# Angle attention's node state and table in five parts at the head of each pass, and layer norms in five parts on ACT and DVE

## The reference

```python
h = relu(layernorm(x));  x = x + weighted_means(h)      # L0
h = relu(layernorm(x));  x = x + graph_conv_with_experts(h)   # L1
h = relu(layernorm(x));  x = x + angle_attention(h)     # L2, four passes
h = relu(layernorm(x));  x = x + graph_attention(h)     # L3, three passes

def layernorm(x):                     # over the 256 features, no gain and no shift
    m = mean(x); v = var(x)
    return (x - m) / sqrt(v + 1e-5)

def agnn_layer(h, src, dst, beta):    # one pass of L2, a relu behind each
    h_norm = h * rsqrt(sum(h * h) + 1e-16)
    logits = beta * sum(h_norm[src] * h_norm[dst])
    ex = exp(logits - segment_max(logits, dst)[dst])
    alpha = ex / (segment_sum(ex, dst)[dst] + 1e-16)
    return segment_sum(alpha * h[src], dst)
```

## Time and profile before

| what | value |
|---|---|
| median of 3 runs | 10534.61 us (10525.16 to 10535.69) |
| the profiled execution's own time | 10475.0 us |
| its span, from the first to the last instruction | 10473.3 us |
| busy: PE, DVE, ACT, POOL | 61%, 49%, 29%, 52% of the span |
| angle attention | from about 3992 to 7501 us |
| mean granted TensorE clock | 0.823 of full speed |

### The profile page before, as it was taken

How to read it: one execution, slowest core, us unless ns; L and a number is a source line. 1 busy time by engine, 2 the same in 40 slices (tenths; PEclk the granted TensorE clock), 3 DMA queues, 4 the chain that set the end, 5 groups by cost and what they waited for, 6 DMA issues and landing times. The chain is left out here.

```text
span 10473.3 us, 149576 instructions
## 1 busy us (share of the span) xinstructions
PE 6360.4 (61%) x33521; PEld 5067.1 (48%) x33705; DVE 5160.9 (49%) x13884; ACT 2997.1 (29%) x7335; POOL 5395.9 (52%) x5498
## 2 busy tenths in 40 slices
PE   0004334434453954885787788678568867776876
PEld 0003324433343843664665566466445545554554
DVE  7002223341113226555556555555667757775777
ACT  0000000000001212333333333333245545553554
POOL 2766666646652123554554555455255545563554
PEclk9996666666676977998998899899788888898888
DMA  3201113343343952334334334333333343342334
GB/s 134 73 8 40 39 40 86 86 58 99 92 72 119 364 185 63 82 83 72 83 82 70 86 82 82 73 81 83 47 85 76 78 68 73 77 79 65 79 76 68
DMA packets 615211, 886.77 MB, mean 85 GB/s; under 512 B 285857, under 2 KB 423587, under 8 KB 613834
## 3 DMA queue, kind: packets, MB, share of 16 engines
q0 software_dynamic: 241344, 609.84, 26.8%
q1 hardware_dynamic: 373770, 275.99, 8.7%
HBM read 757.80 MB, written 134.33 MB: 85 GB/s over the span
## 5 line engine op out<-in xcount | busy, mean ns | idle before, releaser
L1569 POOL DMA_INDIRECT hs<-tab_agnn,rec x1952 | 1877.0, 962 | 1700.9 <-issue 535.0
L2010 POOL DMA_INDIRECT hs<-tab_gat,rec x1464 | 1514.7, 1035 | 1135.7 <-DVE msg L2084 522.1
L1633 DVE CUSTOM_DVE_ANT_0 prod<-psG,hs 128x256 f32<-128x256 f32 x1952 | 836.0, 482 | 992.2 <-remote 528.1
L1692 PE MATMUL psG<-HN,ohT 128*128 x3904 | 1103.9, 428 | 94.4 <-DVE lg L1633 76.8
L2042 DVE TENSOR_REDUCE mt<-psL 128x2 f32<-128x1024 f32 x732 | 871.9, 1219 | 463.8 <-remote 245.0
L1709 PE MATMUL psV<-hs,pr 128*128 128x258 f32 x3904 | 1005.4, 404 | 2.9 <-DVE acc L1616 2.8
L1692 PEld LDWEIGHTS psG<-HN,ohT 128*128 128x128 f32 x3904 | 779.1, 212 | 241.8 <-DVE lg L1633 102.0
L2175 PE MATMUL psV<-msg,oh 128*128 128x260 f32 x2928 | 821.1, 429 | 16.1 <-issue 13.8
L1709 PEld LDWEIGHTS psV<-hs,pr 128*128 128x128 f32 x3904 | 758.0, 205 | 103.7 <-DVE acc L1616 4.4
L661 PE MATMUL psT<-ident,oh 128*128 128x128 f32 x488 | 120.0, 393 | 1128.4 <-issue 792.6
L1648 ACT ACTIVATE prT<-cand,mn 128x512 f32<-128x512 f32 x488 | 352.4, 722 | 1485.8 <-DVE mn L1594 1091.4
(11 more groups left out here) (320 smaller groups left out, 12565.0 us busy)
## 6 DMA issues: line engine op xcount, KB each, us to landing
w<-in_L_gnn_w SPq DMA_DIRECT2D x224, 512.0 KB, 5.7
fwd_d<-acc SPq DMA_DIRECT2D x10, 3172.0 KB
fw<-fwd_d SPq DMA_DIRECT2D x122, 260.0 KB
hs<-tab_agnn,rec POOLq DMA_INDIRECT x1952
hs<-tab_gat,rec POOLq DMA_INDIRECT x1464
rec<-rec_d SPq DMA_DIRECT2D x1220, 8.0 KB
b<-in_L_gnn_b SPq DMA_DIRECT2D x113, 128.0 KB, 6.5
x<-xbuf SPq DMA_DIRECT2D x112, 128.0 KB, 6.2
```

Of the source, the lines that this page charges most:

```text
L1569: nc.gpsimd.indirect_dma_start(out=hs[:, j, g, :], out_offset=None, in_=k.tab_agnn, in_offset=bass.IndirectOffsetOnAxis(ap=rec[:, j, g, 0: ...
L1633: ins = V.tensor_tensor_reduce(prod[:, h2, g, :], psG[:, bank(j2, half), m, :], hs[:, j2, g, 0:D], hs[:, j2, g, D:D + 1], 0.0, ALU.mult, A ...
L1692: mm = nc.tensor.matmul(psG[:, bank(j1, half), m, :], ohT[:, j1 % 2, 2 * half + m, :], pick(HN, b, slice(None)).rearrange("p a c -> p (a c ...
L2010: nc.gpsimd.indirect_dma_start(out=hs[:, j, g, :], out_offset=None, in_=k.tab_gat, in_offset=bass.IndirectOffsetOnAxis(ap=rec[:, j, g, 0:1 ...
```

## The change

The layer norm's instructions are cut into five parts of five blocks each, and DVE and ACT work at different parts at a time. The subtraction of the mean is gone as a sweep of its own: ACT squares `X - mean` with the mean as its bias, one instruction per block (25 of 256 columns), and DVE makes `(X - mean) * rstd` in one instruction per block with both as scalars. The norm can write somewhere else than into `k.H`.

In angle attention the head and the tail of a pass are no blocks of their own any more. What the tail did for the state, and what the head did for the norm, the table and `HN`, stands in front of each engine's part of the pipeline, in five parts. The product and the maximum with 0 are one instruction. `k.acc` and `low` are cleared by POOL, a part of `k.acc` when DVE has read it. SP stores the table in five parts and goes on to the records without waiting; POOL waits for all five before it gathers, and PE for all of `HN`. The layer norm ahead of angle attention writes into `k.acc`, with ones as the sum of exponentials, so that the first pass begins as the others do. Behind the fourth pass the state is made once more in front of the addition to `k.X`.

```diff
@@ class Norm
+        self.root = sb("root", [P, NB], F32)
     def on_vector(self, dve):
-        c = Chain(dve, q.ln, n * 6)
-        Hf = k.H[:, :, 0:D]
-        c.done(nc.vector.tensor_reduce(mean[:, :], k.X[:, :, :], AX.X, ALU.add))
-        c.done(nc.vector.tensor_scalar(mean[:, :], mean[:, :], 1.0 / D, None, ALU.mult))
-        c.done(nc.vector.tensor_tensor(Hf, k.X[:, :, :], b3(mean[:, :], D), ALU.subtract))
-        dve.wait_ge(q.ln_sq, n + 1)
-        c.done(nc.vector.tensor_reduce(var[:, :], sq[:, :, :], AX.X, ALU.add))
-        c.done(nc.vector.tensor_scalar(var[:, :], var[:, :], 1.0 / D, LN_EPS, ALU.mult, ALU.add))
+        for c in range(NORM_PARTS + 1):
+            if c < NORM_PARTS:
+                V.tensor_reduce(mean[:, norm_part(c)], k.X[:, norm_part(c), :], AX.X, ALU.add).then_inc(q.ln_sum, 1)
+            if c >= 1:
+                dve.wait_ge(q.ln_sum, n * NORM_PARTS + c)
+                V.tensor_scalar(mean[:, norm_part(c - 1)], mean[:, norm_part(c - 1)], -1.0 / D, None, ALU.mult).then_inc(q.ln_mean, 1)
+        for c in range(NORM_PARTS):
+            dve.wait_ge(q.ln_sq, n * NORM_PARTS + c + 1)
+            ins = V.tensor_reduce(var[:, norm_part(c)], sq[:, norm_part(c), :], AX.X, ALU.add)
+        c = Chain(dve, q.ln, n * 3)
+        c.done(ins)
+        c.done(V.tensor_scalar(var[:, :], var[:, :], 1.0 / D, LN_EPS, ALU.mult, ALU.add))
         dve.wait_ge(q.ln_sd, n + 1)
-        c.done(nc.vector.reciprocal(rstd[:, :], mean[:, :]))
-        nc.vector.tensor_tensor(sq[:, :, :], Hf, b3(rstd[:, :], D), ALU.mult).then_inc(q.ln_h, 1)
+        c.done(V.reciprocal(rstd[:, :], root[:, :]))
+        for c in range(NORM_PARTS):
+            for b in range(NB)[norm_part(c)]:
+                ins = V.tensor_scalar(sq[:, b, :], k.X[:, b, :], mean[:, b:b + 1], rstd[:, b:b + 1], ALU.add, ALU.mult)
+            ins.then_inc(q.ln_out, 1)
     def on_scalar(self, act):
-        act.wait_ge(q.ln, n * 6 + 3)
-        nc.scalar.activation(sq[:, :, :], k.H[:, :, 0:D], ACT.Square).then_inc(q.ln_sq, 1)
...
+        for c in range(NORM_PARTS):
+            act.wait_ge(q.ln_mean, n * NORM_PARTS + c + 1)
+            for b in range(NB)[norm_part(c)]:
+                ins = nc.scalar.activation(sq[:, b, :], k.X[:, b, :], ACT.Square, bias=mean[:, b:b + 1])
+            ins.then_inc(q.ln_sq, 1)
+        act.wait_ge(q.ln, n * 3 + 2)
+        nc.scalar.activation(self.root[:, :], var[:, :], ACT.Sqrt).then_inc(q.ln_sd, 1)
+        for c in range(NORM_PARTS):
+            act.wait_ge(q.ln_out, n * NORM_PARTS + c + 1)
+            nc.scalar.activation(self.to[:, norm_part(c), 0:D], sq[:, norm_part(c), :], ACT.Relu).then_inc(q.ln_h, 1)
@@ def attention_by_angle
-    layernorm(nc, k)
+    layernorm(nc, k, k.acc)
...
+                nc.vector.memset(k.acc[:, :, D + 1], 1.0)
...
-            with nc.Block() as block:
-
-                @block.scalar
...
+            def state_on_vector(dve):
+                V.tensor_scalar(ss[:, :], k.acc[:, :, D + 1], 1e-16, None, ALU.add).then_inc(s_node, 1)
+                dve.wait_ge(s_node, layer * 2 + 1)
+                V.reciprocal(rn[:, :], ss[:, :]).then_inc(s_node, 1)
+                dve.wait_ge(s_node, layer * 2 + 2)
+                for n in range(NC + 2):
+                    if n < NC:
+                        c = part(n)
+                        V.scalar_tensor_tensor(out=k.H[:, c, 0:D], in0=k.acc[:, c, 0:D], scalar=0.0, in1=b3(rn[:, c], D),
+                                               op0=ALU.max, op1=ALU.mult).then_inc(s_h, 1)
+                    if 1 <= n <= NC:
+                        c = part(n - 1)
+                        dve.wait_ge(s_sq, nc_of(n))
+                        V.tensor_reduce(ssq[:, c], HN[:, c, :], AX.X, ALU.add).then_inc(s_sum, 1)
+                        dve.wait_ge(s_sum, nc_of(n))
+                        V.tensor_scalar(ssq[:, c], ssq[:, c], 1e-16, None, ALU.add).then_inc(s_eps, 1)
+                    if n >= 2:
+                        dve.wait_ge(s_sd, nc_of(n - 1))
+                        V.reciprocal(k.H[:, part(n - 2), D], root[:, part(n - 2)]).then_inc(s_norm, 1)
+                dve.wait_ge(s_norm, nc_of(NC))
+                V.tensor_scalar(rnb[:, :], k.H[:, :, D], betas[:, ds(layer, 1)], None, ALU.mult).then_inc(s_rnb, 1)
+                dve.wait_ge(s_rnb, layer + 1)
+                for n in range(NC):
+                    V.tensor_tensor(HN[:, part(n), :], k.H[:, part(n), 0:D], b3(rnb[:, part(n)], D), ALU.mult).then_inc(s_hn, 1)
+                dve.wait_ge(s_mem, layer * (NC + 1) + (NC + 1))
+
+            def state_on_scalar(act):
+                for n in range(NC + 1):
+                    if n < NC:
+                        act.wait_ge(s_h, nc_of(n + 1))
+                        nc.scalar.activation(HN[:, part(n), :], k.H[:, part(n), 0:D], ACT.Square).then_inc(s_sq, 1)
+                    if n >= 1:
+                        act.wait_ge(s_eps, nc_of(n))
+                        nc.scalar.activation(root[:, part(n - 1)], ssq[:, part(n - 1)], ACT.Sqrt).then_inc(s_sd, 1)
+
+            def state_on_pool(pool):
+                nc.gpsimd.memset(low[:, :], BIG).then_inc(s_mem, 1)
+                for n in range(NC):
+                    pool.wait_ge(s_h, nc_of(n + 1))
+                    nc.gpsimd.memset(k.acc[:, part(n), :], 0.0).then_inc(s_mem, 1)
+                pool.wait_ge(s_tab, nc_of(NC) * 16)
+
+            def state_on_sync(sp):
+                for n in range(NC):
+                    sp.wait_ge(s_norm, nc_of(n + 1))
+                    sp.dma_start(rows(k.tab_agnn[0:NP, :])[:, part(n), :], k.H[:, part(n), 0:W_AGNN]).then_inc(s_tab, 16)
...
                 @block.tensor
                 def _(pe):
+                    pe.wait_ge(s_hn, nc_of(NC))
...
-            with nc.Block() as block:
-
-                @block.vector
-                def _(dve):
-                    c = Chain(dve, s_end, layer * 4)
...
+                c.done(V.scalar_tensor_tensor(out=HN[:, :, :], in0=k.acc[:, :, 0:D], scalar=0.0, in1=b3(rn[:, :], D),
+                                              op0=ALU.max, op1=ALU.mult))
+                c.done(V.tensor_tensor(k.X[:, :, :], k.X[:, :, :], HN[:, :, :], ALU.add))
```

More of the change, by code:

```diff
@@ L451, in on_scalar, with layernorm @@
         sq, mean, var = self.sq, self.mean, self.var
-        act.wait_ge(q.ln, n * 6 + 3)
-        nc.scalar.activation(sq[:, :, :], k.H[:, :, 0:D], ACT.Square).then_inc(q.ln_sq, 1)
[L454 to L460, removed]
+        for c in range(NORM_PARTS):
[8 more added lines that the diff above has]
+            nc.scalar.activation(self.to[:, norm_part(c), 0:D], sq[:, norm_part(c), :], ACT.Relu).then_inc(q.ln_h, 1)
+def layernorm(nc, k, to=None):
     with ExitStack() as ctx:
-        norm = Norm(nc, k, lambda n, s, d: ctx.enter_context(nc.sbuf_tensor(tagged(nc, n), s, d)))
+        norm = Norm(nc, k, lambda n, s, d: ctx.enter_context(nc.sbuf_tensor(tagged(nc, n), s, d)), to)
         with nc.Block() as block:
@@ L1460, in attention_by_angle @@
         rn = sb("rn", [P, NB])
+        ssq = sb("ssq", [P, NB])
+        root = sb("root", [P, NB])
         rnb = sb("rnb", [P, NB])
@@ L1504, in _ @@
                 nc.vector.memset(k.H[:, :, D + 1:W_AGNN], 1.0)
+                nc.vector.memset(k.acc[:, :, D + 1], 1.0)
+        NC = 5
+        part = lambda n: slice(n * (NB // NC), (n + 1) * (NB // NC))
         with nc.Fori(0, L2_LAYERS) as layer:
-            with nc.Block() as block:
-                @block.scalar
[L1510 to L1513, removed]
-                @block.vector
-                def _(dve):
[L1517 to L1520, removed]
-                    c.done(nc.vector.tensor_reduce(ss[:, :], HN[:, :, :], AX.X, ALU.add))
-                    c.done(nc.vector.tensor_scalar(ss[:, :], ss[:, :], 1e-16, None, ALU.add))
-                    dve.wait_ge(s_sq, layer * 2 + 2)
-                    c.done(nc.vector.reciprocal(k.H[:, :, D], rn[:, :]))
-                    c.done(nc.vector.tensor_scalar(rnb[:, :], k.H[:, :, D], betas[:, ds(layer, 1)], None, ALU.mult))
-                    c.mark(nc.vector.tensor_tensor(HN[:, :, :], k.H[:, :, 0:D], b3(rnb[:, :], D), ALU.mult))
-                @block.sync
-                def _(sp):
-                    sp.wait_ge(s_node, layer * 5 + 3)
-                    sp.dma_start(rows(k.tab_agnn[0:NP, :]), k.H[:, :, 0:W_AGNN]).then_inc(s_tab, 16)
-                    sp.wait_ge(s_tab, layer * 16 + 16)
@@ L1720, in _ @@
                     pipeline(pe, step, 5, numbers=blocks)
-            with nc.Block() as block:
-                @block.vector
-                def _(dve):
-                    c = Chain(dve, s_end, layer * 4)
-                    V = nc.vector
-                    c.done(V.tensor_scalar(ss[:, :], k.acc[:, :, D + 1], 1e-16, None, ALU.add))
-                    c.done(V.reciprocal(rn[:, :], ss[:, :]))
-                    c.done(V.tensor_tensor(HN[:, :, :], k.acc[:, :, 0:D], b3(rn[:, :], D), ALU.mult))
```

(11 more changed lines are left out.)

33 lines of the change are left out of this document (29 added, 4 removed).

## The result

The changed kernel took 10423.06 us (median of 4 runs, 10392.32 to 10437.46) against 10533.26 of the kernel before in the same session (4 runs, 10525.16 to 10535.69): ratio 0.989, 95% interval 0.9862 to 0.9918, so 110 us faster. The forecast was 10425. The two profiled executions differ by only 51.6 us in span: the one of the kernel before took 10475.0, 58 us under its median, the one of the kernel after 10423.42, at its median, and 40 us of the gap lie in the four loops.

The account below looks back on a forecast made before the run. No engine bounds the whole span; the work is a chain of phases. Savings of 45 + 5.5 + 49.8 + 2.0 + 7.3 = 109.6 us, taken from the median 10534.6, gave 10425, range 10385 to 10478.

Parts of the forecast that it names:

- The norms: Three exposed layer norms: 24.5 us each instead of 39.7, taken as 15 saved each, 45 in all.
- The first norm: Norm beside POOL's scatter of records: 5.5 us from ending long scatters; 11.7 more for POOL, or nothing if DMA sets the pace.
- The heads: Starts of the angle attention passes: 16.6 us saved in each of three, 49.8 in all, and 2.0 in the first.
- E to S: From the end of a pass's last accumulation to DVE's first instruction of the next head: 4.9 us instead of 19.5.
- the step that put its start behind HN: First gather of a pass: POOL could start at S+22.3, but HN's two-input instructions put it at S+24.3.
- PE's new wait: PE's wait for HN in the head: holds back only first transposes, which need oh, behind HN on DVE; no cost.
- The fill: Pipeline filling after a pass's first gather: stays 33 us long and shifts with the heads.
- rival B: DVE pauses before the first oh: up to 16.6 us lost in three heads, 10 in the first; 10485; chance 0.17.
- Rival C: No DVE pause in the fill: up to 15 us more saved in three heads; 155 in all, 10380; chance 0.12.
- The tail: After the last angle attention pass: one DVE sweep (6.82) and a barrier (0.48) go, 7.3 us saved.
- Rival D: Angle loops fetch code at each turn, 2.5 us times 76, 190 us: 80 slower, 10615; chance 0.05.
- Rival F: Parts of the heads don't overlap, ACT loading tables twice per part: 5 us a head, 20 in all; 10445; chance 0.05.

Follow-up runs that it names:

- session 1: Follow-up session with four kernels: before 9341.55 us, norms alone ratio 0.9963, heads alone 0.9926, the whole change 9217.63, ratio 0.9865.
- run with one part: Changed kernel with only the first of five parts of HN made, four fifths of the scaled state left out: 9224.28 us, a single run.
- run with the later wait: Changed kernel with PE's wait for HN moved behind its load of block numbers, to the second loop step: 9226.14 us, ratio 0.9873.
- the later wait and HN shared: Changed kernel with PE's wait for HN behind its number loads and ACT making the last two of HN's five parts: 10297.99 us, ratio 0.9895.
- sessions 1 and 2: The first two follow-up sessions; the kernel before took 9341.55 and 9346.38 us in them.
- the first pair: The original profiled executions, kernel before against changed kernel: 10475.0 and 10423.42 us.
- session 3: Follow-up session repeating both kernels unchanged: changed 10295.72 us against 10402.23 before, ratio 0.9888.

## Why the prediction was right, and where it was not

**The norms** (45 forecast) gave 44.1. Two parts were off by more than 0.2 us. The 25 tensor_scalar take 8.17 us, 0.33 each, not the 0.27 of the earlier trace rows; nearer the other bound of the step, 0.34. Of the 1.4 us that this costs, 0.8 came back ahead of it: the five sums with their scalings took 7.5 us, not 8.2, so the first tensor_scalar starts 15.5 us into the norm, not 16.3.

**The first norm** (5.5) gave nothing: the last scatter starts at 716.9 against 716.3. The term's premise was right, POOL did gain; that the gain reaches the end of the scatter was wrong. The scatters of 6.42 and 7.18 us are gone; the line's rows in the kernel after (minimum, median, maximum in ns):
```profile
L415 POOLq MOVE  x392: 29/700/703, 178.7 to 718.3; - x196
L415 POOL DMA_INDIRECT rec_d<-R x392: 969/971/1149, 179.6 to 716.9; - x196
...
  DMA rec_d<-R: 19.1, 4
```
The longest scatter is 1.15 us, but POOL then waits 19.1 us for the scatters' own transfers, where it waited 10.5 before. In session 1 these waits went from 10.9 to 22.6 us, by just the 11.7 that the two long scatters had cost: the transfers set the pace, the step's lower bound. The rule that I weighed there, of the Trainium skill (SBUF — State Buffer, "SBUF: two separate sides"), would have the 25 tensor_scalar lock POOL too. This trace shows next to nothing of it: while they ran, from 200.96 to 209.12, POOL's scatters took 0.99 to 1.06 us, 0.02 to 0.09 more than beside nothing; as each lasts 0.33 us, a hold as short as one of them isn't excluded. What stood beside the long scatters of the earlier trace rows was an instruction with two inputs in SBUF. The same section of the Trainium skill names that form too, against a GpSimd instruction that reads SBUF, so it covers what the prediction took the trace to add. With HN, of that form, the trace agrees: the gather ends 0.8 us after HN's last part, whenever it began.

**The heads** (49.8 and 2.0 forecast) gave 59.8 and 5.3 up to the gather, and gave some of it back behind it. E to S was 3.4, not 4.9: I had taken the jump's cost over whole from the earlier trace rows; it was 1.5 us less a pass, and why, no run tells. The gather came at S+22.7 to S+23.5 by pass and run, not S+24.3: the step that put its start behind HN was wrong. HN holds its end, and that costs 0.5 us, as the run with one part showed. The 5.3 of pass 1 are some 4 us from S on (from S+27.2 to S+23.3) and 1.4 ahead of it.

**PE's new wait** was costed at nothing, "holds back only its first transposes, which need oh". As to when PE starts, that step failed. Behind the wait stands the load of the block numbers, 2.88 us, and then the transposes: 3 us late, of which 1 reaches the product, since the gathered rows come late as well. The run with the later wait shows it: from gather to product its four passes take 30.3 us, after in session 1 33.8 and before 29.0. That is 3.5 of the +4.9 in the table. In the time of the pass it costs nothing where loops take 700 us, for the same table has -4.6 in the next row; where they take 780, it may be what brings the pause forward.

**The fill** was forecast to shift unchanged. It did in session 1, where gather to first accumulation takes 132.3 us in four passes against 132.0. Where loops last 780 us it grew by 10 to 13 us, 5 to 11 of them behind the first product. That is rival B in its direction (DVE pauses earlier), but only a tenth to a fifth of the 60 us that B put on it: in the profile the earlier pause also ends earlier, in mid-burst, and a second, shorter one follows. With the later wait and HN shared this growth was gone. Rival C, no pause, is what sessions 1 and 2 show in both kernels, so it was never the change's to bring.

**The tail** (7.3) gave 7.1.

**Rival D** falls: loops of the same length, and in the kernel after two instruction packets within 5 us at the outer jump (4841 to 4846) and none in 680 us of loop (4973 to 5653), as in the earlier trace rows. The rule of the Trainium skill (Runtime: NRT & Kernel Launch, "Instruction fetch mechanics") that a branch out of the window stalls stays untested: no packet came in the stretch of loop looked at. **Rival F** falls too: ACT loads a table before the first Square and before the first Sqrt of each head and never between the parts.

**The sum** was 109.6. With the rows down to the first accumulation the table gives 102 in the first pair (116.3 - 2.6 - 10.8 - 0.6), 117 in session 1 and 108 in session 3. The medians differ by 110, 124 and 107. So in the session of the forecast the term that came out too small (the heads, by 13) and those that came out too large or were missed (the first norm 5.5, PE's load and the fill 13) nearly cancel: the mechanism of the big terms was right, the closeness to 110 was luck. Setting the difference against the median, not against one profiled execution, was right: the profiled pair alone gives 52.

## What to carry to other kernels

Splitting a chain of full-width sweeps into parts paid here what the sum of the parts said, within a tenth, because the other engines' work on a part is shorter than the longest engine's: time that engine's chain, and put the others beneath it. When a wait is added to an engine, look up what stands behind it in program order, register loads too, which busy time doesn't show; then follow the delay to the first result that others wait for, since it may be absorbed on the way, as here in session 1. Check a gain in a head against the balance of all phases of two profiles: four loops that scatter by some 10 us each hid 40 of a gain of 110.

## What had not been expected of the hardware

The same program takes 9341 or 10402 to 10533 us, 11 to 13% apart, by session. The heads, tails and exposed norms are the same to 1 us in both, and only pipelined stretches differ (a loop of angle attention 700 or 780 us). A matmul of psG takes 379 ns at the median in both; the mean granted clock over the whole span is 0.82 of full speed in the one and 0.86 in the other, 0.91 to 0.93 and 0.94 to 0.95 within a loop. Register and semaphore instructions differ far more. The row of L415 above has its register moves on POOL at 29, 700 and 703 ns; the same line of the changed kernel in session 1:
```profile
L415 POOLq MOVE  x392: 29/29/29, 178.7 to 689.4; - x196
L415 POOL DMA_INDIRECT rec_d<-R x392: 969/972/1149, 179.6 to 703.9; - x196
```
Session 1 has no move over 500 ns on POOL and no semaphore instruction over 500 ns on SyncE; the kernel before in the first pair has 246 and 93. Whether any of these is the cause or a sign of something else, no run could tell. The long pause of DVE in the fill is seen only in the sessions with loops of 780 us.

A load of block numbers into PE's registers takes 2.88 us, one on DVE 4.06; each is longer than any instruction on a part in the head (1.49).

The first gather of a pass, begun beside a part of HN, ended 0.8 us after that part in 28 passes of 28, and took 1.15 to 1.92 us for it, against 0.95 alone. The scatters of 6.42 and 7.18 us, begun 1.3 and 0.5 us into a sweep of two inputs, ended 0.8 us after it too; the one begun with the sweep, 0.02 us into L441 (192.49), took its 0.97.
